# The norm ahead of the experts, made inside the experts' loop for 61 of 64 units

## The reference

```python
x = x + _L0_xattn_ref(_layernorm(x, axis=-1), ctx_1024, ctx_1024, ...)
x = x + _L0_ffn_ref(_layernorm(x, axis=-1), ...)        # 8 experts, 2 per sequence, exact GELU
x = x + _L1_xattn_ref(ctx_1024, ctx_1024, _layernorm(x, axis=-1), mask, 16, ...)
x = x + _L1_ffn_ref(x, W_fc, W_proj)                    # relu squared, then spikes
...
def _layernorm(x, axis=-1, eps=1e-05):
    m = jnp.mean(x, axis=axis, keepdims=True)
    v = jnp.var(x, axis=axis, keepdims=True)
    return (x - m) / jnp.sqrt(v + eps)
```

## Time and profile before

| | us |
|---|---|
| median of 3 runs | 3878.18 (3874.96 to 3878.55) |
| span of the profiled execution | 3869.9 |
| preparation and first attention | 0 to 943 |
| preparation of the experts | 943 to 996 |
| experts' loop | 996 to 2382 |
| second attention and spiking | 2382 to 3870 |

### The profile page before, as it was taken

How to read it: one execution, slowest core, us unless ns; L and a number is a source line. 1 busy time by engine, 2 the same in 40 slices (tenths; PEclk the granted TensorE clock), 3 DMA queues, 4 the chain that set the end, 5 groups by cost and what they waited for, 6 DMA issues and landing times. The chain is left out here.

```text
span 3869.9 us, 134428 instructions
## 1 busy us (share of the span) xinstructions
PE 3678.2 (95%) x47408; PEld 2870.0 (74%) x47408; DVE 3088.5 (80%) x5266; ACT 2207.4 (57%) x4529; POOL 2200.5 (57%) x3316
## 2 busy tenths in 40 slices
PE   5999999995799999999999996999999999999999
PEld 4777777773688888888888884566666668888888
DVE  4888888885778777778777775798888977777777
ACT  3777777775444444444444442577677765555554
POOL 5666666664245443333333334466666667887777
PEclk9999999997899999999999998899999999999999
DMA  4677777774332322222222224799999952232322
GB/s 130 197 204 207 214 209 209 205 213 154 102 85 79 84 68 74 66 70 69 68 72 68 72 66 90 158 211 216 211 217 208 215 151 80 75 77 75 79 75 72
DMA packets 834241, 502.59 MB, mean 130 GB/s; under 512 B 262037, under 2 KB 824408, under 8 KB 833480
## 3 DMA queue, kind: packets, MB, share of 16 engines
q1 hardware_dynamic: 832680, 493.49, 50.5%
q0 software_dynamic: 928, 0.49, 0.1%
HBM read 251.27 MB, written 214.96 MB: 120 GB/s over the span
## 5 line engine op out<-in xcount | busy, mean ns | idle before, releaser
L1556 ACT ACTIVATE phase_spare<-phase_loop_hid,phase_b1T 128x128 f32<-128x128 f32 x2048 | 586.1, 368 | 710.9 <-PE phase_loop_hid L193 702.2
L1129 DVE TENSOR_REDUCE phase_loop_mx<-phase_loop_score 128x8 f32<-128x1024 f32 x512 | 625.4, 1222 | 98.5 <-PE phase_loop_score L882 91.0
L1522 PE MATMUL phase_loop_moe_y<-phase_w,phase_spare 128*128 x2048 | 693.6, 379 | 0.1
L1037 ACT ACTIVATE phase_loop_pt<-phase_loop_scoreT 128x1024 f32<-128x1024 f32 x448 | 458.6, 1024 | 268.3 <-PE phase_loop_scoreT L916 265.8
L1524 PE MATMUL phase_loop_moe_y<-phase_w,phase_spare 128*128 x2048 | 558.2, 273 | 0.0
L191 PE MATMUL phase_loop_hid<-phase_loop_moe_h,all_w_first_hi 128*128 128x128 f16 x2048 | 449.2, 219 | 0.0
L192 PE MATMUL phase_loop_hid<-phase_loop_moe_h,all_w_first_hi 128*128 128x128 f16 x2048 | 449.1, 219 | 0.0
L192 PE MATMUL phase_loop_hid<-phase_loop_moe_h,phase_w_hi 128*128 128x128 f16 x2048 | 449.1, 219 | 0.0
L193 PE MATMUL phase_loop_hid<-phase_loop_moe_h,all_w_first_lo 128*128 128x128 f16 x2048 | 449.1, 219 | 0.0
L193 PE MATMUL phase_loop_hid<-phase_loop_moe_h,phase_w_lo 128*128 128x128 f16 x2048 | 449.1, 219 | 0.0
L191 PE MATMUL phase_loop_hid<-phase_loop_moe_h,phase_w_hi 128*128 128x128 f16 x2048 | 449.0, 219 | 0.0
(11 more groups left out here) (293 smaller groups left out, 11038.9 us busy)
## 6 DMA issues: line engine op xcount, KB each, us to landing
qk_scratch<-phase_loop_qk SPq DMA_DIRECT2D x192, 256.0 KB, 3.4
phase_loop_cin<-in_ctx SPq DMA_DIRECT2D x128, 256.0 KB, 4.6
x_scratch<-phase_loop_x SPq DMA_DIRECT2D x128, 256.0 KB, 3.1
h_scratch<-phase_loop_hr SPq DMA_DIRECT2D x128, 256.0 KB, 3.7
phase_loop_qS<-qk_scratch SPq DMA_DIRECT2D x384, 64.0 KB, 2.8
phase_loop_kS<-qk_scratch SPq DMA_DIRECT2D x384, 64.0 KB, 2.4
ks_scratch<-ct_scratch SPq DMA_DIRECT2D x384, 64.0 KB, 2.4
all_w_first_lo<-ks_scratch SPq DMA_DIRECT2D x128, 192.0 KB, 4.0
```

Of the source, the lines that this page charges most:

```text
L1037: act.activation(pt[n % len(pt)][:, :, :], score_t_bank[:, :].rearrange("p (j n) -> p j n", j=HB2), ACT.Exp, scale=exp_scale).then_inc(s_e ...
L1129: v.tensor_reduce(to, score_bank[:, :].rearrange("p (h j n) -> p h j n", h=2, j=CH), AX.X, ALU.max).then_inc(s_mx.sem, 1)
L1522: pe.matmul(o[:, :], hh[n % NH][:, j, :], row, start=half == 0 and j == 0, stop=False, skip_group_check=True)
L1556: i = act.activation(hf[n % NF][:, j, :], hid(u, n)[:, j * S:(j + 1) * S], ACT.Gelu, bias=w["b1"][:, bass.ds(e * HB + (4 * half + j), 1)], ...
```

## The change

For units 0 to 2 all stays as it is. For units 3 to 63 the first attention no longer makes the norm ln1: `norm1_stats`, `rstd1`, `rows1`, `norm1` and `store_h` return at once. The experts' loop makes it instead, with buffers of its own, in steps 1 to 62, where v counts the moved units from 0 and stands for unit v + 3:

- SyncE: `load_later(v)` loads x1 of unit v + 3 in step v, `store_h(v)` stores its halves in step v + 2, behind `load` and ahead of `stack_k`. `load(u)` waits for the h of its unit.
- VectorE: `stats_later(v)` in step v + 1, behind split(1).
- GpSimd: `factors_later(v)` in step v + 1, behind `gates` and ahead of `factors`; `rows_later(v)` in step v + 2, first of all.
- ScalarE: `norm_later(v)` in step v + 1, between gelu(2) and gelu(3).

```diff
@@ -58,6 +58,7 @@
 KEPT = 3e38
 LOOP = 4
+NORMED = 3
 CUT_BY_MIN, CUT_BY_PRODUCT = (1,), (3,)
@@ -482,6 +483,7 @@
     units = n_seq // PAIR
+    normed = NORMED if first else units
     NP = 4
     DEPTH = 12
     NX = 10
@@ -638,6 +640,8 @@
                     d_x1.inc(sp.dma_start(x1v[u.no], x1[u.slot][:, :, :]), u)
                 def store_h(u):
+                    if u.no >= normed:
+                        return
                     s_hr.wait(sp, u)
                     d_h.inc(rows_out(sp, h_out[u.no], hr[u.slot][:, :, :, :]), u)
@@ -719,7 +723,7 @@
                 for s in range(2):
                     end = Unit(0, units - 2 + s)
                     d_x1.wait(sp, end)
-                    d_h.wait(sp, end)
+                    d_h.wait(sp, Unit(0, normed - 2 + s))
                     if first:
                         d_ct.wait(sp, end)
@@ -1103,13 +1113,16 @@
                     else:
                         d_x.wait(v, u)
                     d_x1.wait(v, u.back(2))
-                    ln1.s_xn.wait(v, u.back(2))
+                    if u.no - 2 < normed:
+                        ln1.s_xn.wait(v, u.back(2))
                     v.scalar_tensor_tensor(out=x1[u.slot][:, :, :],
                                            in0=ring["o"][:, :].rearrange("p (a n) -> p a n", a=PAIR),
                                            scalar=p2(-Y_X - W_X), in1=u.of(xin)[:, :, :], op0=ALU.mult,
                                            op1=ALU.add).then_inc(s_x1.sem, 1)
                 def norm1_stats(u):
+                    if u.no >= normed:
+                        return
                     s_x1.wait(v, u)
                     ln1.stats(v, u, x1[u.slot])
@@ -1373,6 +1386,17 @@
         d_ks = k.dsig("m_ks", 6)
         ln = Norm(k, "ln0b", c, k.sem("ticks_v"), k.sem("ticks_g"), late["valid"], products=1)
         s_xrh, s_xr, s_xb = k.sig("m_xrh"), k.sig("m_xr"), k.sig("m_xb")
+
+
+        later = units - NORMED
+        xl = two("moe_xl", [P, PAIR, D], F32)
+        hr = two("moe_hr", [P, PAIR, 2, D], F16)
+        ln1 = Norm(k, "ln1a", c, ln.ticks_v, ln.ticks_g, None, products=1)
+        d_xl, d_hs = k.dsig("m_xl"), k.dsig("m_hs")
+        s_hrh, s_hr = k.sig("m_hrh"), k.sig("m_hr")
+
+        def is_later(v):
+            return v.no < later
         s_m1, s_ge, s_hi, s_lo, s_m2 = (k.sig(f"m_{n}", NC) for n in "m1 ge hi lo m2".split())
         s_t, s_x2 = k.sig("m_t", 5 * PAIR), k.sig("m_x2", PAIR)
         s_b2, s_b2x = k.sem("m_b2"), k.sem("m_b2x")
@@ -1387,8 +1411,20 @@
         with nc.Block() as block:
             @block.sync
             def _(sp):
+                def load_later(v):
+                    if is_later(v):
+                        ln1.s_xn.wait(sp, v.back(2))
+                        d_xl.inc(sp.dma_start(xl[v.slot][:, :, :], x1v[v.no + NORMED]), v)
+
+                def store_h(v):
+                    if is_later(v):
+                        s_hr.wait(sp, v)
+                        d_hs.inc(rows_out(sp, io["h"][v.no + NORMED], hr[v.slot][:, :, :, :]), v)
+
                 def load(u):
                     s_m1.wait(sp, u.back(2))
+                    if u.no >= NORMED:
+                        d_hs.wait(sp, u.back(NORMED))
                     d_h.inc(columns_in(sp, hT[u.slot][:, :, :, :], io["h"][u.no]), u)
                     if u.no == 0:
                         sp.dma_start(w["b2"], io["L0_ffn_b2"].rearrange("(o e) d -> o (e d)", o=1).to_broadcast([P, EXP * D])
@@ -1422,7 +1458,8 @@
                         for i, part in enumerate((hi, lo, hi)):
                             src = part.rearrange("(b h d) n -> h d b n", h=2, d=DK)[hh]
                             d_ks.inc(sp.dma_start(io["ks"][u.no][hh, i * DK:(i + 1) * DK], src), u)
-                run_steps(sp, [(3, store_late), (2, load_late), (0, load), (1, stack_k), (3, store_rows), (3, store)], units, 3)
+                run_steps(sp, [(3, store_late), (2, load_late), (0, load), (0, load_later), (2, store_h), (1, stack_k),
+                               (3, store_rows), (3, store)], units, 3)
                 for s in range(2):
                     d_o.wait(sp, Unit(0, units - 2 + s))
                     d_xr.wait(sp, Unit(0, units - 2 + s))
@@ -1471,7 +1508,17 @@
                     g.tensor_copy(lh[:, :], lw[:, :]).then_inc(s_lh.sem, 1)
                     s_lh.wait(g, u)
                     g.tensor_tensor(ll[:, :], lw[:, :], lh[:, :], ALU.subtract).then_inc(s_ll.sem, 1)
-                run_steps(g, [(1, gates), (2, factors), (2, rows), (2, bias), (2, halves)], units, 3)
+                def factors_later(v):
+                    if is_later(v):
+                        ln1.rstd(g, v)
+                        ln1.shift(g, v)
+
+                def rows_later(v):
+                    if is_later(v):
+                        d_hs.wait(g, v.back(2))
+                        ln1.split_rows(g, v, hr[v.slot], s_hrh, s_hr)
+                run_steps(g, [(2, rows_later), (1, gates), (1, factors_later), (2, factors), (2, rows), (2, bias),
+                              (2, halves)], units, 3)
             @block.tensor
             def _(pe):
@@ -1562,7 +1609,12 @@
                 def norm(u):
                     s_xr.wait(act, u.back(1))
                     ln.apply_act(act, u, x2[u.slot])
-                run_steps(act, [(1, read)] + [(1, gelu(n)) for n in range(6)] + [(2, norm)]
+                def norm_later(v):
+                    if is_later(v):
+                        s_hr.wait(act, v.back(1))
+                        ln1.apply_act(act, v, xl[v.slot])
+                run_steps(act, [(1, read)] + [(1, gelu(n)) for n in range(3)] + [(1, norm_later)]
+                          + [(1, gelu(n)) for n in range(3, 6)] + [(2, norm)]
                           + [(1, gelu(n)) for n in range(6, NC)], units, 3)
             @block.vector
@@ -1636,9 +1688,16 @@
                     s_x2.wait(v, u)
                     ln.stats(v, u, x2[u.slot])
+                def stats_later(x):
+                    if is_later(x):
+                        d_xl.wait(v, x)
+                        ln1.stats(v, x, xl[x.slot])
+
                 tasks = [(1, read)]
                 for n in range(NC):
                     tasks.append((1, split(n)))
+                    if n == 1:
+                        tasks.append((1, stats_later))
                     if n == 0:
                         tasks.append((1, top))
                     if n == 5:
```

## The result

The changed kernel takes 4078.11 us (median of 4 runs, 4074.39 to 4078.84), the kernel before 3876.57: ratio 1.0519, 95% interval 1.0506 to 1.0533, that is 201.5 us slower. The forecast was 4068, +190. The profiled execution spans 4077.0 us; 3869.9 was the span before, so 207.1 us are to be found.

The account below looks back on a forecast made before the run. TensorE was taken to set both loops, only just in the experts' loop, where a ring of waits would take over. 3878 + 210 (+3.5 us per unit, 60 steps) - 20 = 4068 us, range 3996 to 4139.

Parts of the forecast that it names:

- Its ring: Experts' loop: chain of waits through VectorE, GpSimd and ScalarE, from 21.68 us per unit to 25.1, against a 21.61 repeat.
- T0: Experts' loop: the end of the second MAX8 of `top` on VectorE, where each unit's count starts.
- The detour through ScalarE: Experts' loop: norm_later waits for factors_later, delaying gelu(3) and so split(3) from 5.24 to 7.6 us after T0, +2.36.
- The port: Experts' loop: GpSimd's cast and subtract in rows_later slow VectorE's split(7) by 1.0 us per unit, bounds 0.15 and 1.7.
- The rear rstd: Experts' loop: rstd of the rear norm on GpSimd meets split(4) and split(5), costing 0.1 us, bounds 0 to 0.4.
- The statistics: Experts' loop: stats_later takes 1.07 to 1.2 us on VectorE, falls on its idle 1.17 and alone costs nothing.
- SyncE hidden: Experts' loop: issuing load_later and store_h, about 0.4 and 0.6 us, stays hidden; if not, 1 us per unit.
- The removal: First attention: leaving out 61 of 64 norms saves 20 us, bounds 9 and 26, mostly in long units and drain.
- the eight long ones: First attention: 8 units that split expert weights ahead lose waits of 1.2 us each, 10 us, bounds 0 and 13.1.
- Rival 1: Experts' loop: added work fits in the holes, repeat stays 21.61 if the ring stays under it; 3858 us, chance 0.06.
- Rival 2: Experts' loop: norm_later does not hold ScalarE, only statistics and port lengthen the ring, to 22.7; 3924 us, chance 0.08.
- Rival 3: Experts' loop: TensorE's clock falls too through idle gaps, 26.5 us per unit; about 4150 us, chance 0.10.

Follow-up runs that it names:

- the two ablations: From the changed kernel: the loop makes no norm either, 3853.58 us; or the first attention makes all 64 norms again while the loop still makes 61, 4095.34 us.

## Why the prediction was right

Its ring, measured term by term with the same arithmetic on the unit shown (T0 = 1733.96 + 0.24 = 1734.20):

| term | predicted | measured |
|---|---|---|
| T0 to split(3) | 7.6 | 7.24 |
| to the end of the rear statistics | 2.13 | 2.14 |
| to ScalarE's rear norm | 2.93 + 0.1 | 3.33 |
| rear norm | 1.09 | 1.09 |
| to add(0), with the port's share | 5.10 + 1.0 | 6.34 |
| to the next T0 | 5.19 | 5.18 |
| sum | 25.1 | 25.32 |

- *What bounds the loop* was right: the ring of 21.68 with 1.17 of slack beside a TensorE of 21.61. Nothing else explains that the same instructions cost 201 us in one order and gain 23 in another.
- *The detour through ScalarE* is the largest term, predicted at 2.36 and measured at 2.00 in the unit (7.24 - 5.24), 2.26 when taken away. It was over-sized by 0.36: the gates end 3.22 after T0 and not 3.42, the four factors take 1.68 and not 1.73, and gelu(3) starts 0.09 before the end of the norm. ScalarE stood still for 4.11 us and not 3, since gelu(2) was over 0.97 after T0 and not 2.2; on the ring only the end of that wait counts.
- *The port* was taken at 1.0 and is 1.24 in the unit (6.34 - 5.10), 1.15 when taken away. Between the bounds 0.15 and 1.7, near the value that was read from split(6). The Trainium skill, "SBUF — State Buffer", section "SBUF: two separate sides", has "the other fully blocks", and the rows of split(7) agree with it: each half ends only after GpSimd's instruction has. What was wrong is the step from there to 1.7. A half waits only for the part of the other instruction that is still to come, less the 0.14: 1752.53 - 1751.99 - 0.13 = 0.41 for the first, 1753.87 - 1752.85 - 0.14 = 0.88 for the second, 1.29 together, of which 1.24 reach the ring. 1.0 came near by analogy with split(6) and not by a reckoning of these overlaps. The row that the prediction set against the page, stays odd: that half ended at 1097.85, before L1469 did (1098.09).
- *The rear rstd* is the term that was mis-sized: 0.1 taken, 0.40 measured (3.33 - 2.93), the very end of its bounds. GpSimd's chain of five takes 3.01 us (1743.80 to 1746.81) instead of 2.61 (1716.43 to 1719.04 before), since split(4), split(5) and add_bias(0) now run beside it. Its stretched instructions end just behind one of VectorE's: L419 at 1745.78, 0.06 after split(5)'s second half, L428 at 1746.81, 0.06 after add_bias(0).
- *The statistics* on the idle 1.17: right, and the row at 1736.17. *SyncE hidden*: as far as the views go, right: no engine names a DMA as what it waits for in the loop, and the run with the store last shows no gain. The gate logits' wait (at most 0.9) names nothing and stays unexplained.
- The errors of the terms, -0.36, +0.24 and +0.30, cancel in part, and that much of the closeness is luck; the mean repeat is 25.27 against 25.1, so the 60 steps brought (25.27 - 21.61) x 60 = 220 instead of 210. The last two units take 20.9 and 20.8, where 21.6 was forecast; why is open.
- *The removal* was taken at -20: 16.4 at the barrier of the changed kernel, 17 to 24 by the two ablations. The 9 us behind the last L1107 were right to 0.1. Followed unit by unit, the eight long ones gave 10.3 us, where 10 were predicted: six are plain now, the first is as before, and the last still took 14.26, because it now waits for a DMA. TensorE's row in it:

```profile
591.32 0.40 PE L924 MATMUL phase_loop_scoreT<-phase_loop_qS,phase_loop_kS 51*128 51x128 f16 x8 [1.02 <-DMA phase_loop_qS<-max_scratch]
```

  What was missed is what was given back: the first L1118 starts 1.8 us later than the first L1107, and the last five units of the drain take 1.5 us more. The runs with the same first attention differ by 5.6 us at the next block's first DMA (921.55 to 927.14), so these two may be scatter; they weren't followed up. The extra 1 us in the drain did not show.
- *Rival 1* was wrong for this order, but its condition, a ring that stays under TensorE's repeat, was the right one: in the version with the rows behind the bias the ring just reaches it, the loop stays at 21.62 and the time is 3858, the number that the rival gave. *Rival 2* has its own run: with the norm behind gelu(4) the repeat is 23.01 and the time 3934, against its 22.7 and 3924; the 0.3 are again the stretched rear rstd (0.4) and the port (0.2), less 0.3 by which the statistics took under 1.2. *Rival 3* did not come: the granted clock is 1.00 over 1400 us with gaps of up to 1.4 us. The rule of the Trainium skill, "TensorE: Matmul & The Clock Gate", section "Part 1: The HAM clock gate (the "warmup" mystery)", is that idleness takes the array down; with the gaps of this loop the trace shows no fall.

## What to carry to other kernels

Before work is moved into a loop, walk one repeat through all engines in program order, write down its length and its slack, and place each new instruction where nothing on that ring queues behind its wait; shares of busy time (57% of ScalarE here) say nothing about it. A wait costs what is queued behind it, once per repeat, when the ring has no slack: here the place of one 1.09 us instruction in ScalarE's order was worth 144 us, and the same work in another order made the kernel 23 us faster than before. Contention between VectorE and GpSimd is priced in the same way: lay the two timelines over each other, count for each instruction the part of the other that it has to wait out, and then ask whether it is on the ring. 1.2 us of it cost 1.15 on the full ring and nothing on the one with slack.

## What the runs showed of the hardware

- VectorE's splits and GpSimd's large instructions (128x512) wait for each other in full. The one that starts inside the other ends 0.13 to 0.14 less than its own length after the other's end: split halves of 0.41 and 0.69 end 0.28 and 0.55 after a cast, a subtract or the bias; a cast of 0.61 ends 0.47 after a split.
- Small GpSimd instructions, two numbers per partition, wait for a split in the same way but do not hold one: the power at L413 took 0.69 us beside add(1) and 1.16 beside split(2), ending 0.57 after it; L419 took 0.47 instead of 0.20, L428 0.40 instead of 0.20. In a chain of five this made 0.40 us. The power at L1446 (1710.83 to 1711.52 in the kernel before) left the split half inside it at 0.43.
- add(1), which reads TensorE's result, neither waits nor holds: in the run with the store last it takes its 1.52 us (from 1744.52) with a cast of 0.60 beside it.
- TensorE at 92% busy, with three gaps per unit of 0.2 to 1.4 us, kept the clock at 1.00 from 1100 to 2500 us.
